# A fused attention and gated feed-forward kernel on one core: key turns behind the second gate half, fewer waits ahead of matmuls

## The reference

```python
xn = layernorm(x)                          # x: 4 batches of 512 rows of 512
qkv = xn @ w_qkv; q, k, v = split(qkv)     # 16 heads of 32
q = rope(rmsnorm(q, q_gamma)); k = rope(rmsnorm(k, k_gamma))
s = (softmax(causal(q @ k.T / sqrt(32))) @ v) @ w_out
gate = silu(xn @ dequant(wq_gate).T)       # 1408 hidden columns, (w - 128) * scale
up   = xn @ dequant(wq_up).T
g = silu((gate * up) @ dequant(wq_down).T)
out = x + s * g
```

## Time and profile before

| what | value |
|---|---|
| time before, median of 3 | 674.71 us (673.88 to 675.73) |
| the profiled execution | 673.6 us, its span 671.9 us |
| TensorE (matmul) busy | 651.6 us, 97% |
| VectorE busy | 530.2 us, 79% |
| ScalarE busy | 457.5 us, 68% |
| GpSimd busy | 412.5 us, 61% |
| mean granted TensorE clock | 0.996 |

### The profile page before, as it was taken

The page is one execution under the profiler, slowest core; times in us unless marked ns, Lnnn a source line. Parts: engine busy times, 40 slices in busy tenths (PEclk is TensorE's granted clock), DMA queues, the critical chain, the costliest instruction groups (busy, mean ns, idle before and its releaser), DMA issues.

```text
span 671.9 us, 12576 instructions
## 1 busy us (share of the span) xinstructions
PE 651.6 (97%) x3690; PEld 550.7 (82%) x3690; DVE 530.2 (79%) x1345; ACT 457.5 (68%) x1013; POOL 412.5 (61%) x591
## 2 busy tenths in 40 slices
PE   8889999999999999999999999999999999988997
PEld 6768888888888888888888888888888887766886
DVE  6786888989787888798878887978788787546584
ACT  3588887777676777777767677767776787643441
POOL 7968687687565767685766677766657684510000
PEclk9999999999999999999999999999999999998999
DMA  8536436442534341335333321245372516459884
GB/s 278 198 138 216 157 107 196 118 119 61 135 99 126 112 112 49 110 97 126 110 110 106 97 85 45 58 124 153 110 217 74 157 49 172 128 176 335 307 308 144
DMA packets 62592, 94.40 MB, mean 140 GB/s; under 512 B 12093, under 2 KB 24381, under 8 KB 62397
## 3 DMA queue, kind: packets, MB, share of 16 engines
q1 hardware_dynamic: 62524, 93.59, 45.6%
HBM read 59.09 MB, written 25.82 MB: 126 GB/s over the span
## 4 chain that ended last, share of the span: by engine, by line
PE 81%; DVE 6%; POOL 5%; ACT 3%; issue 3%; DMA 2%; SPq 0%; DVEq 0%; ACTq 0%; POOLq 0%
PE bank L1467 23%; PE bank L1364 17%; PE bank L1404 9%; PE bank L1443 6%; PE bank L1425 6%; PE bank L1389 5%; PE bank L1493 5%; PE bank L1492 4%; PE bank L1376 4%; POOL rr L641 1%; DVE bank L1100 1%; DMA stage<-w_qkv 1%; DVE pp L1078 1%; POOL pp L661 1%; POOL on L669 1%
## 5 line engine op out<-in xcount | busy, mean ns | idle before, releaser
L661 POOL TENSOR_SCALAR_AFFINE_SELECT pp<-pp 128x256 fp32r<-128x256 f32 x256 | 107.1, 431 | 145.4 <-DVE pp L1078 145.2
L1100 DVE CUSTOM_DVE_ANT_0 bank<-bank,msk_w 128x128 f32<-128x128 f32 (+3 forms) x256 | 121.3, 509 | 38.2 <-PE bank L1425 37.9
L1078 DVE TENSOR_TENSOR pp<-pf,pp 128x512 fp32r<-128x512 f32 (+1 forms) x192 | 133.1, 693 | 6.3 <-ACT pp L792 5.8
L641 POOL TENSOR_TENSOR rr<-ss,half 128x8 f32<-128x8 f32 x64 | 108.7, 1699 | 16.3 <-DVE ss L1046 16.2
L1364 PE MATMUL bank<-wq,xnt_h 128*128 128x384 f32 x512 | 111.8, 340 | 2.7 <-DVE qn L1058 2.2
L791 ACT ACTIVATE pf<-bank 128x512 f32<-128x512 f32 (+1 forms) x192 | 100.5, 523 | 13.6 <-PE bank L1389 10.7
L792 ACT ACTIVATE pp<-bank 128x512 fp32r<-128x512 f32 (+1 forms) x192 | 100.7, 525 | 0.0
L1467 PE MATMUL bank<-xnt_h,wgu 128*128 128x512 f32 x352 | 99.1, 403 | 0.1
L1404 PE MATMUL bank<-pp,va 128*65 128x512 f32 (+3 forms) x512 | 97.1, 310 | 1.0 <-POOL pp L661 1.0
L1467 PE MATMUL bank<-xnt_l,wgu 128*128 128x512 f32 x352 | 96.6, 396 | 0.0
L1364 PEld LDWEIGHTS bank<-wq,xnt_h 128*128 128x128 f32 x512 | 88.5, 188 | 6.2 <-issue 4.4
(11 more groups left out here) (90 smaller groups left out, 1206.3 us busy)
## 6 DMA issues: line engine op xcount, KB each, us to landing
wgu<-wg_dram SPq DMA_DIRECT2D x66, 256.0 KB, 3.1
hf_dram<-g SPq DMA_DIRECT2D x44, 256.0 KB, 3.2
hf_raw<-hf_dram SPq DMA_DIRECT2D x16, 512.0 KB, 6.7
wg_dram<-wgu SPq DMA_DIRECT2D x22, 256.0 KB, 3.1
xr<-x SPq DMA_DIRECT2D x16, 256.0 KB, 5.1
oh<-oraw SPq DMA_DIRECT2D x64, 64.0 KB, 2.0
ol<-oraw SPq DMA_DIRECT2D x64, 64.0 KB, 2.0
s_dram<-s_sb SPq DMA_DIRECT2D x16, 256.0 KB, 3.1
```

The lines of the kernel that those rows point to most:

```text
L641: pool.tensor_tensor(rr[:, s, :], ss[:, s, :], half[:], ALU.pow).then_inc(rr_ok, 1)
L661: op = pool.affine_select(pp[:, :, a:a + P], pp[:, :, a:a + P], [[0, 2], [1, P]], ALU.is_ge, 0.0, base=0, channel_multiplier=-1)
L1078: dve.tensor_tensor(pl[:, tile], pf[:, tile], ph[:, tile].bitcast(F32), ALU.subtract).then_inc(pl_ok, 1)
L1100: op = dve.tensor_tensor_reduce(bank[:, a * w:(a + 1) * w], bank[:, a * w:(a + 1) * w], msk_w[:, N - w:N], 1.0, -3.0e38, ALU.add, ALU.max, ...
```

## The change

- On TensorE the key turn of every beat moves behind `gate_half(half_at(c, 1))`. It stood ahead of it: behind the last maxima in most beats, behind `project(..., 1)` in late-turn beats.
- On TensorE several waits are left out that others imply (of `project` three of four, of each `turn` one of two, of `maxima` one of two, `xt_hi` in two places), and the wait for the weights of a half is a call of its own, `weights_there`, made earlier in the beat.
- On ScalarE `square` and `k_evac` change places, so that `k_evac` ends the beat.
- Two layer norms of batch 1 move one beat earlier (4 to 3, 5 to 4).
- Behind the beats SyncE issues the loads 9, 10, 11 ahead of the last head group's denominators, and `high` and `low` of 9, 10, 11 stand earlier in ScalarE's and VectorE's lists.

```diff
@@ ln_at
-                b, t = 1, {4: 0, 5: 1, 7: 2, 8: 3}.get(c)
+                b, t = 1, {3: 0, 4: 1, 7: 2, 8: 3}.get(c)
@@ SyncE, behind the beats
+            for v in range(9, 12):
+                load_hf(v)
             den_in(LAST)
-            load_hf(9)
             den_back(LAST)
-            load_hf(10)
-            load_hf(11)
@@ ScalarE, beat
+                if there(j + 7, NB):
+                    square(j + 7, (c + 7) % 2, (c + 7) // 4 % VR, (c + 7) % 4)
                 if turned:
                     k_evac(j + 5, (c + 5) // 4 % 2, (c + 5) % 4)
-                if there(j + 7, NB):
-                    square(j + 7, (c + 7) % 2, (c + 7) // 4 % VR, (c + 7) % 4)
@@ ScalarE, behind the beats
             outer(0, 0)
+            high(9)
+            high(10)
             outer(0, 1)
-            high(9)
+            high(11)
             o_high(LAST, G - 1)
-            high(10)
             outer(0, 2)
-            high(11)
@@ VectorE, behind the beats
             low(9)
+            low(10)
             scaled(0, 2)
+            low(11)
+            scaled(0, 3)
             o_low(LAST, G - 1)
-            low(10)
-            scaled(0, 3)
             finish(0, 0)
             finish(0, 1)
-            low(11)
@@ TensorE, project
-                        pe.wait_ge(xt_hi, 4 * b + t + 1)
                         pe.wait_ge(xt_lo, 4 * b + t + 1)
...
-                    wait(pe, sq_ok, used)
-                    wait(pe, vh_ok, used)
-                    wait(pe, vl_ok, used)
+                    if n <= 6:
+                        wait(pe, vl_ok, used)
                     wait(pe, qn_ok, used)
@@ TensorE, turn
-                pe.wait_ge(tl_ok, n + 1)
-                wait(pe, tq_ev if a else tk_ev, n + a)
+                if a:
+                    pe.wait_ge(tq_ev, n + 1)
+                else:
+                    if n <= RING:
+                        wait(pe, tk_ev, n)
+                    pe.wait_ge(tl_ok, n + 1)
@@ TensorE, maxima
-                        pe.wait_ge(tq_ev, n + 1)
                         pe.wait_ge(tk_ev, n + 1)
@@ TensorE, new, and gate_half
+            def weights_there(qq):
+                if qq is None:
+                    return
+                b, q, s = qq // HALVES, qq % HALVES, qq % RING
+                if b == 0:
+                    pe.wait_ge(wgc_ok, q + 1)
+                else:
+                    wait(pe, wg_in[s], 16 * len([v for v in range(HALVES, qq + 1) if v % RING == s]))
...
-                    wait(pe, xt_hi, 4 * b + 4)
                     wait(pe, xt_lo, 4 * b + 4)
-                if b == 0:
-                    pe.wait_ge(wgc_ok, q + 1)
-                else:
-                    wait(pe, wg_in[s], 16 * len([v for v in range(HALVES, qq + 1) if v % RING == s]))
@@ TensorE, beat
                 if attend:
                     scores_t(r, c, 0)
+                weights_there(half_at(c, 0))
...
                 gate_half(half_at(c, 0))
+                weights_there(half_at(c, 1))
...
                 banks(SM_C)
-                if not late_turn(c):
-                    turn_k()
                 if proj:
                     project(r, c + 7, 1)
                 if c in DOWN_MID:
                     down(0, *DOWN_MID[c][1])
-                if late_turn(c):
-                    turn_k()
                 gate_half(half_at(c, 1))
+                turn_k()
                 for t, m0, m1 in DOWN_AT.get(c, ()):
                     down(0, t, m0, m1)
                 if attend:
                     p_v(r, c, 0)
```

More of the change, by code:

```diff
@@ L1614, in fill @@
                 project(0, 3, 0)
+                weights_there(0)
                 gate_half(0)
@@ L1621, in fill @@
                 turn(0, 0, 1)
+                weights_there(1)
                 gate_half(1)
@@ L1631, in fill @@
                 turn(0, 2, 1)
+                weights_there(2)
                 gate_half(2)
@@ L1647, in fill @@
                 maxima(0, 3, (4,))
+                weights_there(3)
                 gate_half(3)
```

## The result

| | before | after |
|---|---|---|
| median | 675.22 us (673.88 to 676.14, 4 runs) | 702.48 us (701.67 to 703.21, 4 runs) |
| ratio, 95% interval | | 1.0405 (1.0381 to 1.0429) |
| profiled execution, its span | 673.6, 671.9 us | 701.96, 700.2 us |
| TensorE's granted clock, mean | 0.996 | 0.998 |

A forecast was written before the change was run, and what follows sets the result against it. TensorE, busy for 97% of the span, was taken to bound the kernel. Terms +31.8 + 0.5 - 1 - 0.4 - 5 = +25.9 us on the median 674.7 gave 700.6 us, range 690 to 709.

The forecast's parts named there:

- The chain behind the gate half: Late-turn key copy and `t_high` precede the tanh on ScalarE; tanh 1.32 us later, up multiply's predecessor on VectorE 1.33 later.
- G: Start of the first matmul behind the gate half, where the moved key turn now starts; 306.55 us in the beat examined.
- The wait of TensorE: Ahead of the up half in 30 beats: 1.01 us each, 30.3, plus 1.5 for `o_high`; +31.8 us.
- The slack of 0.07: Average us by which the up half could start earlier: three tight beats to one with 0.25 slack.
- Elsewhere: Other beats with a turn: small waits at maxima and new-batch transposes; +0.5 us, bounds 0 to +3.
- Fewer waits: Some 370 waits dropped on TensorE over the beats, at most 3 ns each; -1 us, bounds 0 and 4.4 gained.
- Waits for weights: Made at most half a beat earlier, weights requested two beats ahead, so still met; 0, at worst +1 us.
- layer norms: Beat 6's 0.37 us stall at the projection may go with norms a beat earlier; -0.4, bounds -0.8 and +0.5.
- Behind the beats: Earlier loads 9 to 11 remove TensorE's waits of 1.71 and 2.02 us and a lower clock; -5, bounds -6 and 0.
- the tanh wasn't delayed: Rival: key copy and `t_high` fit into ScalarE's idle time, only other terms count; 668.3 us, chance 0.06.
- only the key copy stood in its way: Rival: `t_high` gets ahead of the key copy, multiply 0.70 later, TensorE waits 0.38; 680 us, chance 0.04.
- The lower clock: Part of a rival: TensorE's clock falls in the new gaps, or a second wait joins; 710 to 720 us, chance 0.08.

The follow-up runs named there:

- e1: Changed kernel with the key turn, and the order of `square` and `k_evac`, as before the change: 669.62 us, ratio 0.9927.
- e2: Kernel before with only the key turn moved behind the gate half and `k_evac` behind `square`: 709.81 us, ratio 1.0518.
- e3: Changed kernel with ScalarE's key copy moved behind the next beat's `t_high` copies, still ahead of the tanh: 692.15 us, ratio 1.0255.
- e9: Changed kernel with the key copy behind the next beat's `t_high` only in the 30 beats with a tanh there: 682.09 us, ratio 1.011.
- e10: Changed kernel with the wait for a half's weights made directly ahead of each half again: 704.68 us, ratio 1.0449.
- e6: Kernel before with only TensorE's waits changed (some left out, those for weights made earlier): 670.76 us, ratio 0.9948.
- e7: Kernel before with only the two layer norms a beat earlier: 673.7 us, ratio 0.9994.
- e5: Kernel before with only the edits behind the beats (loads 9 to 11 first, their splits moved): 674.93 us, ratio 1.0004.
- e12: Changed kernel with the key turn back in its old place and the small transfers put between loads 9, 10 and 11: 666.79 us, ratio 0.989.
- e11: Kernel before with TensorE's waits changed and the two layer norms a beat earlier: 670.41 us, ratio 0.9941.
- e4: Changed kernel with ScalarE's key copy behind the next beat's tanh, or behind `t_high` where no tanh opens the beat: 691.9 us, ratio 1.0254.
- e8: Changed kernel with the key turn back and batch 2's first three splits ahead of multiplies that wait for output transfers: 670.13 us, ratio 0.9936.

## Why the prediction was right, by its steps

**The chain behind the gate half** (key copy, `t_high`, tanh, multiply) was forecast at G + 0.45, 0.95, 1.57, 2.37 and stands at 0.45, 0.94, 1.55, 2.34. e1 and e2 show that the place of the turn, with its key copy, decides, e3 and e9 that TensorE pays for what stands ahead of the tanh. In the three beats with an `o_high` the tanh comes at G + 2.07, the forecast 0.5 more.

**The wait of TensorE** was forecast at 1.01 us a beat, 31.8 in all with `o_high`. Measured by the beats' starts: 10.14, 9.68 and 9.84 us over the three stretches, 29.7 in all. e2, the turn alone, shows the term as it was meant: 10.98, 10.57 and 10.67, that is 32.2, against 31.8. Two things were not in the sum. The up half starts 0.05 behind the multiply, no longer 0.15; e10 shows it to be the other wait, worth 2.5 us over the 30 beats, which is the whole distance from 32.2 to 29.7. And two waits are new: the gate half for the up multiply (line 1128), 4.1 us in 12 beats, which the turn no longer covers and VectorE reaches 1.3 us later; and the transposed maxima (line 1433), 1.2 us in six beats. How much of their 5.3 us is on the path was not separated. e2's list has the second one too (1.1 us), and its 32.2 is only 0.4 above the forecast, so it can't be much.

The slack of 0.07 was right on average, its make-up not quite: from the multiply's end to the up half the kernel before has 0.15 us in 11 of the 30 beats, 0.16 to 0.21 in 13 and 0.4 in six, so the large slack comes once in five beats and not once in four.

**Elsewhere** +0.5, bounds 0 to +3: in the changed kernel the offsets grow by 0.12 up to beat 12 (counted from beat 0 by 0.02), by 0.26 and 0.30 over beats 23 to 28 and 39 to 44, 0.7 in all, with the layer norms' gain in it. In e2, where the norms stand as before, the same stretches grow by 0.84, 0.36 and 0.35 (the first counted from beat 0): 1.5, within the bounds but three times the value taken.

**Fewer waits** had the wrong reason, and by the medians the wrong size: -1 by 3 ns for each of 370. e6 gives -3.2 us. In its trace 1.5 of it is there by beat 55, in the tight beats; in the changed kernel, where every up half is held, the weights' wait alone is worth 2.5, about 0.1 each. Beats with slack gain nothing. At an equal clock e6 has -2.0 to -2.6; the remainder goes with a lower clock that came less often in its runs.

**Waits for weights** 0, and **layer norms** -0.4: no reader waits for weights, and e7 moves -0.65 us in the trace and nothing that the times tell.

**Behind the beats** was mis-sized: -5, and it is the step that failed. From beat 55 (+30.34) to the matmul that starts at 613.67 before and 638.58 after (+24.91) the gain is 5.4, as in the sum of the waits and the clock. Then 1.8 comes back as the wait at 648.29 (+26.75 at `down(2, 0)`), and 1.5 at the end, where the last multiplies wait for output transfers (last matmul +26.87, end +28.35). Kept: 2.0. The bounds had the cause (transfers busy throughout, "part may come back as a wait for batch 2"), the value taken didn't. What the prediction didn't have is the small store that gates SyncE: with three loads ahead of it it takes longer than in any kernel without them. Alone (e5) the edit is worth 0, and with the small transfers between the loads (e12) the sum of all but the turn is 7.8 us under before.

**Sum.** The fewer waits and the layer norms lie within the beats, so the terms up to beat 55 go together: 31.8 + 0.5 - 1 - 0.4 = 30.9 was forecast, 29.7 + 0.7 = 30.4 came. Behind them it was -5 and came to -2.0. That gives +28.3 between the profiled spans for +25.9. That the first part fits so well is partly luck. From beat 0 to beat 55 the turn alone costs 33.8 us (e2) and not 32.3, and the rest of the change takes 3.5 back and not 1.4; the two misses have opposite signs.

The range doesn't follow from the terms' own bounds: with each at its slowest (beats +39, elsewhere +3, fewer waits 0, weights +1, norms +0.5, behind the beats 0) they reach +43.5, not +38. The result lies far from that end. Of the rivals, the changed kernel's profile rules out that the tanh wasn't delayed and that only the key copy stood in its way. The lower clock, which would have taken it to 710, did not come in the 1 us gaps: the granted clock is 1.00 over the whole stretch from 45 to 694 us.

## To carry over

An instruction that waits late on an in-order engine pulls everything behind it in that engine's list: before moving its producer, list what stands behind the consumer and when each must be done, and look for chains that come back with no wait listed, since their slack may be zero. A wait costs nothing in a queue that runs ahead and about 0.1 us in front of an instruction that is held. Loads moved ahead of a small round trip on the same queue can give back what they win: in the changed kernel 3.4 of 5.4 us came back, in e5 all of it. With the small transfers between the loads (e12) none did. Try that order first.

## What the runs showed of the hardware

The round trip of the small store, from its issue to the next queue entry that waits for it, was 4.40 to 4.75 us in seven kernels with three loads ahead of it (4.45 in the changed kernel, 4.75 in e1) and 6.32 in the eighth, e5. In the old order, one load behind it, it was 3.26 (before), 3.05 (e2), 2.92 (e7) and 1.42 (e6 and e11), and in e12, with one load ahead and one behind, 1.85. So three loads ahead go with a longer round trip in every case, but the old order varies by a factor of two for a reason that these runs don't show, and one load ahead did no harm. That loads already issued hold up a later small store is what this suggests; the load on the transfers at the same time was not varied apart from that.

The lower clock (1.2 GHz) comes or stays away behind the same waits. All kernels have the same two waits of TensorE near 42 and 43.4 us (1.2 and 0.6 us long); behind them the clock fell for 3.4 us in e1, e4, e8, e10 and e11 and not in the other nine. The granted clock of 43 to 48 was 0.66 in e1 and 1.00 in the changed kernel:

```profile
43.00:48.00 5.00, 4.77 (x18) 3.91 (x18) 3.37 (x11) 2.81 (x6) 3.13 (x3) 0.66 0.39 107
```

```profile
43.00:48.00 5.00, 4.47 (x23) 3.82 (x23) 4.78 (x19) 4.34 (x10) 3.46 (x3) 1.00 0.22 80
```

Within one kernel the time follows it: e12's runs lie from 665.61 us at a mean granted clock of 1.000 to 668.75 at 0.996, those of the kernel before on that chip from 671.90 at 1.000 to 675.79 at 0.993. At 1.000 against 1.000 e12 is 6.3 us faster, and at 0.996 to 0.997 5.9 by the medians (667.97 of three, 673.83 of four), so its gain isn't the clock's. Such a mean is a rough measure: it also counts a lower clock behind the last matmul, where it costs nothing (in the profile before the clock falls at 608.6 for 3.4 us, and again at 670.1, when the last matmul, at 667.35, is done). The Trainium skill (TensorE: Matmul & The Clock Gate, "What's actually happening") has the clock follow how busy the array has lately been; the fall at the end of the 4.24 us wait of e5 agrees, and that equal waits bring it in one execution and not in another is more than the trace explains.
